# Dynamic convolution: the group product of the next input's statistics behind the first twelve products of a sample

## What is computed

```
x = x + L0(_gn(x))          # _gn: mean and variance over groups of 2 channels and all pixels
# L0, per sample:
g     = mean(x, axis=(2, 3))
h     = relu(g @ w1.T + b1)
alpha = softmax(h @ w2.T + b2)            # 4 experts
weff  = einsum('k,koihw->oihw', alpha, experts)
out   = conv3x3(x, weff, padding 1) + alpha @ bias
```

## Time and profile before

| | |
|---|---|
| median of three runs | 2964.48 us (2956.65 to 2966.43) |
| the profiled execution | 2959.49 us, span 2957.7 us |
| TensorE (PE) busy over the span | 2648.0 us, 90% |
| VectorE (DVE) busy | 2111.5 us, 71% |
| ScalarE (ACT) busy | 1329.8 us, 45% |
| GpSimd (POOL) busy | 276.6 us, 9% |
| first product of sample 0 | 35.86 us |
| first instruction of the sweeps on VectorE | 427.82 us |

### The profile page before, as it was taken

How to read it: one execution, slowest core, us unless ns; L and a number is a source line. 1 busy time by engine, 2 the same in 40 slices (tenths; PEclk the granted TensorE clock), 3 DMA queues, 4 the chain that set the end, 5 groups by cost and what they waited for, 6 DMA issues and landing times. The chain is left out here.

```text
span 2957.7 us, 71621 instructions
## 1 busy us (share of the span) xinstructions
PE 2648.0 (90%) x25688; PEld 2419.8 (82%) x25688; DVE 2111.5 (71%) x5086; ACT 1329.8 (45%) x2119; POOL 276.6 (9%) x761
## 2 busy tenths in 40 slices
PE   5888869999999999979988898968999999999990
PEld 3666659999999999975567676758999999999990
DVE  7888847777667677789048888886677767676764
ACT  3767752236652222225546666643225663222220
POOL 1111110000000001131001010110000000000252
PEclk9999989999999999989989999988999999999995
DMA  4333331000000000028536777846000000000299
GB/s 95 86 86 86 85 120 45 0 4 0 0 5 0 0 0 0 0 90 338 119 57 88 109 109 101 116 73 101 0 0 5 0 0 4 0 0 0 44 154 165
DMA packets 674984, 168.85 MB, mean 57 GB/s; under 512 B 663216, under 2 KB 663856, under 8 KB 668464
## 3 DMA queue, kind: packets, MB, share of 16 engines
q1 hardware_dynamic: 545408, 132.08, 21.8%
q10 hardware_dynamic: 129456, 35.12, 6.6%
HBM read 100.07 MB, written 67.11 MB: 57 GB/s over the span
## 5 line engine op out<-in xcount | busy, mean ns | idle before, releaser
L297 PE MATMUL L_conv<-L_x_hi,L_w_hi 128*128 128x248 f32 (+2 forms) x5040 | 1208.4, 278 | 36.8 <-DVE L_w_lo L260 29.1
L297 PE MATMUL L_conv<-L_x_hi,L_w_lo 128*128 128x248 f32 (+2 forms) x5040 | 1201.8, 278 | 0.0
L170 ACT ACTIVATE L_row_b<-S,L_bias 128x256 f32 (+1 forms) x1008 | 513.7, 510 | 1079.5 <-DVE L_x_hi L238 1069.2
L297 PEld LDWEIGHTS L_conv<-L_x_hi,L_w_hi 128*128 128x128 f32 x5040 | 952.9, 189 | 38.1 <-issue 29.3
L297 PEld LDWEIGHTS L_conv<-L_x_hi,L_w_lo 128*128 128x128 f32 x5040 | 954.1, 189 | 0.0
L248 DVE SCALAR_TENSOR_TENSOR S<-L_conv,L_neg_bias,L_row_b 128x256 f32 (+1 forms) x1008 | 487.9, 484 | 441.5 <-PE L_conv L302 435.7
L302 PE MATMUL L_conv<-L_x_lo,L_w_hi 128*128 128x248 f32 (+2 forms) x5040 | 744.0, 278 | 0.0
L302 PEld LDWEIGHTS L_conv<-L_x_lo,L_w_hi 128*128 128x128 f32 x5040 | 655.3, 190 | 0.0
L240 DVE TENSOR_TENSOR L_x_lo<-S,L_x_hi 128x256 fp32r<-128x256 f32 x1016 | 432.5, 426 | 34.7
L238 DVE TENSOR_SCALAR L_x_hi<-S 128x256 fp32r (+1 forms) x1016 | 303.5, 299 | 41.4 <-PEq L47 6.2
L633 PE MATMUL dc_conv<-dc_xz_hi,dc_w_hi 128*128 128x512 f32 x384 | 171.0, 445 | 6.5 <-DVE dc_w_lo L760 6.5
(11 more groups left out here) (210 smaller groups left out, 2802.0 us busy)
## 6 DMA issues: line engine op xcount, KB each, us to landing
dc_raw<-x SPq DMA_DIRECT2D x32, 512.0 KB, 6.6
x_scratch<-dc_raw SPq DMA_DIRECT2D x16, 1024.0 KB, 7.6
at_res<-x_scratch SPq DMA_DIRECT2D x64, 256.0 KB, 6.2
x_scratch<-at_res SPq DMA_DIRECT2D x64, 256.0 KB, 5.4
fs_buf<-x_scratch SPq DMA_DIRECT2D x32, 512.0 KB, 6.3
sh_G<-x_scratch ACTq DMA_DIRECT2D x56, 256.0 KB, 5.3
out<-fs_buf SPq DMA_DIRECT2D x32, 256.0 KB, 4.0
out<-fs_buf ACTq DMA_DIRECT2D x32, 256.0 KB, 4.7
```

The lines of the kernel that those rows point to most:

```text
L170: nc.scalar.activation(row_b[p][:, :, :], line(k, at_step(k, i), p), ACT.Identity, bias=bias[:, k:k + 1]).then_inc(row_b_ready[p], 1)
L297: nc.tensor.matmul(out[:, to, :], w[:, k % SLOTS, s * P:(s + 1) * P], x_hi[p][:, at, :], start=(s == PADJ and n == 0), stop=False)
```

## The change

Within TensorE's order for one sample, the group product of the next input's statistics is issued behind the twelve high products of chunk 0 instead of ahead of them. Nothing else is changed: the same instructions are issued, with the same waits.

```diff
             def sample(t, k):
                 n, u = t * PER + k, k % 2
                 first, last = isinstance(n, int) and n == 0, isinstance(n, int) and n == B - 1
+                products_high(n, 0, u, 0)
+                products_high(n, 0, u, 1)
                 if not last:
                     group(n + 1, INP)
-                products_high(n, 0, u, 0)
-                products_high(n, 0, u, 1)
                 products_low(n, 0, u)
                 if not last:
                     hid(n + 1)
```

## The result

The changed kernel takes 2974.01 us (median of 10 runs, 2968.32 to 2983.89) against 2961.43 for the kernel before (10 runs, 2956.04 to 2966.43). The ratio is 1.0043, interval 1.0032 to 1.0054: slower by 12.6 us. The forecast was 2970 in 2957 to 2981: +5.2 us as the likeliest outcome, and rival 1 (the clock eats the slack) for +12 to +16. The measured ratio lies in the class that had been given a chance of 0.25, slower by more than 0.3%.

What follows compares the result with a forecast made beforehand. The prediction held that ScalarE and VectorE set the convolution's period, with TensorE's stall as slack. It summed +4.7 - 1.0 + 1.5 + 0 = +5.2 us, giving a median forecast of 2970 us, range 2957 to 2981.

Steps and rivals of the forecast that it cites:

- rival 1: Low clock costs time in the 48 products behind the logits and the next twelve: +12 to +16 us; chance 0.22.
- TensorE's stall is slack, the ScalarE and VectorE loop sets the period: Steady samples: the 3 us stall ahead of the group product moves to the gate mean (3.9 us); period effect nothing.
- First sample +4.7: First sample: group product behind twelve products delays VectorE's copy and everything after; +4.7 us, bounds 3.3 to 5.9.
- Waits for the result group, -1: Fewer products ahead of the hidden product shrink VectorE's waits for the result group: -1 us, between nothing and all 2.0.
- Clock +1.5, bounds 0 and 7: Low clock moves behind the hidden product, into work with less room: three deep samples, +1.5 us, bounds 0 and 7.
- The slack: Lateness the next sample's group product can bear without cost: 0.29, 0.15, 0.33 and 0.28, in all 1.05 us.
- Loop turns, 0: Samples 6 and 10: a possible TensorE instruction hole ahead of the twelve products, 0 to 2.2 us per turn; taken as 0.
- The clock's upper bound, +7: Steady samples: worst low-clock loss of 0.55 us beyond the slack in each of thirteen samples, 7 us.
- Rivals 2 and 3: 2: TensorE was the bound, 2930, chance 0.04. 3: first sample's slip absorbed or mis-sized, -1 to +2, about 2965, chance 0.16.

## Why the prediction was right and where it fell short

The range held, the forecast inside it did not: +5.2 us was expected and +12.6 came. That 2970 looks close to 2974 is luck of the starting point, since 2970 was built on a three-run median of 2964.48 for the kernel before, and the ten runs beside the changed kernel gave 2961.43. The range reached the result because it took in rival 1.

- *TensorE's stall is slack, the ScalarE and VectorE loop sets the period.* Right. The stall of 3.0 us moved to L622 as 3.8 us, 2.8 us of added TensorE work per sample cost 1.7 us in all at most, and with the two losses removed the stage is 391.5 against 392.0.
- *First sample +4.7.* Measured 5.2 (the copy) to 5.4 (the period), inside the bounds of 3.3 to 5.9: the twelve products took 4.73 us instead of 4.24, as if two to three more of them ran cold (an estimate from 0.235 and 0.44 us a product, twelve in 2.82 and in 5.27 us in the earlier trace rows). The gate mean came at 46.23, where 44.9 was expected.
- *Waits for the result group, -1.* Wrong in sign. Samples 2 and 12 gained 0.3 and 0.45, but a wait of 0.15 to 0.55 us for it appeared in each of samples 1 to 13, 4.1 us together; the experiment that moved it took 0.3 us off an ordinary period. I had written that the group comes "as late as VectorE wants it", from 6 x 0.44 = 2.6 us. In sample 9 it starts 2.92 us behind the hidden product, and its copy follows 0.45 us later, which was not in that sum.
- *Clock +1.5, bounds 0 and 7.* This is the term that was mis-sized: stage less sample 0 is +6.3, the waits for the result group included, where I had +0.5. The slack (1.05 us in the prediction; one of its terms, from 206.90 to 207.27, is 0.37 and not 0.33) held in ordinary samples: VectorE did not wait for the input's group product in samples 2 to 5, 8, 9, 12 and 13. It failed where the low stretch lasts longer. From the granted clocks of the stretches shown, and the two levels 0.50 and 1.00, I estimate 3.2 us at the low level in sample 9, 6.8 in sample 0 and 7.9 in sample 6. Sample 0 (+2.6 in sample 1) I had not counted at all; its gap of 3.3 us is no longer than the others, and why the low stretch behind it lasts longer stays open. In samples 6 and 10 the gap itself is longer, 5.7 us, because VectorE's wait of 2.3 us at the loop's turn delays the gate mean (the profile shows no releaser; a single packet of the DMA queue for instructions, 0.01 MB, falls inside each of the two waits, before the change as after it, and none in the 10 us ahead of them); their low stretch runs through the logits into the other products (granted clock 0.81 in sample 6), and the next group product is over 1 us late.
- *Loop turns, 0.* No hole of TensorE at the turn; its first product in sample 6 stands 0.20 us, for the low weights, and from 30 to 440 us no wait of its products is without a releaser. The turn costs by way of the clock, +0.6 there and +1.1 in sample 7 (with the gap filled 0.0 in both). That VectorE's own hole would lengthen TensorE's gap was the path that the prediction left out.
- *The clock's upper bound, +7.* The measured +6.3 is near it in size, but not by thirteen samples that lose 0.55 us each. The experiment with fillers and the one with the same fillers emptied show the clock going with what TensorE does in the gap: from the hidden product of sample 9 to its logits it was 1.00 behind 15 products of 512 columns and 0.34 us of idle time, and 0.52 behind 15 of 16 columns and 2.12 us of idle time.
- *Rival 1* happened in price (+12.6 for +12 to +16) and in kind, though its condition (more than 1.05 us lost in most samples) was not met: 5.3 of the 6.3 us lie at samples 1, 6, 7, 10 and 11. Its chance of 0.22 was too low. Rivals 2 and 3 are out.

## What to carry to other kernels

Slack on TensorE was not free to move here: the clock was low behind each of the 15 new gaps (0.50 to 0.53 from the hidden product to the logits in samples 1 to 14, 0.65 in sample 0), so a gap wants to lie ahead of products for which nobody waits, and in the one order tried real work moved into it only moved the gap. When a product is moved behind others, look at the first pass of the loop by itself, since there no earlier pass has hidden anything. And before a difference of a few tenths of a per cent is put down to an edit, compare the stage that was edited, not the total, and learn from an unedited stage how much it scatters.

## What the hardware showed beyond expectation

- Eleven instructions from the hidden product to the logits took 3.27 to 3.30 us at a granted clock of 0.50 to 0.52 behind an idle gap of 2.1 to 5.7 us, and 1.99 at 1.00 with the gap filled.
- Adding some 100 throw-away products to TensorE's code, of 16 to 512 columns, went with 8 to 14 us less in stages that were not edited (2516 to 2522 us against 2530) in the profiled executions of six kernels out of six, and by the medians clearly in five. Part of it is in attention, where TensorE's holes without a releaser fell from six (11.1 us) to three (3.4 to 5.8 us). The cause is not shown.
- 105 products of 16 columns one behind the other took 22.55 us at a granted clock of 0.50, 0.21 us each, while a product of 512 columns took 0.44 at that level.
